# Differential attention: the sum of the two exponentials moves from VectorE to TensorE

## The reference

```python
q1, q2 = split(x @ w_q12);  k1, k2 = split(x @ w_k12);  v = x @ w_v     # each 512 x 128
diff = softmax(q1 @ k1.T * scale) - lam_full * softmax(q2 @ k2.T * scale)
out = diff @ v ;  out / rms(out) * (1 - LAMBDA_INIT)
```

## Time and profile before

| | |
|---|---|
| time, median of 3 runs | 976.47 us (974.27 to 980.98) |
| profiled execution, its own time | 976.01 us |
| span in that profile | 974.3 us |
| mean granted clock of TensorE | 0.942 |
| TensorE matmuls | 825.0 us busy, 85% |
| VectorE | 695.1 us busy, 71% |
| ScalarE | 552.2 us busy, 57% |
| GpSimd | 557.4 us busy, 57% |

### The profile page before, as it was taken

One profiled execution on the slowest core, in us unless ns is written; L12 is line 12 of the kernel. 1 busy time (PEld: TensorE's weight loads), 2 busy tenths in 40 slices (PEclk: granted clock), 3 DMA queues, 4 the chain that ended last, 5 costly groups with the idle time before them and its releaser, 6 DMA issues.

```text
span 974.3 us, 18283 instructions
## 1 busy us (share of the span) xinstructions
PE 825.0 (85%) x6646; PEld 542.3 (56%) x6646; DVE 695.1 (71%) x1441; ACT 552.2 (57%) x1027; POOL 557.4 (57%) x617
## 2 busy tenths in 40 slices
PE   7789998999899999999996877679788859999870
PEld 4356664448644444444443645445556549988870
DVE  5889984014798999999975599988576853654573
ACT  6566665440488887878884743436786544343220
POOL 2500006807188888888332599962077735878872
PEclk9899999999999999999998988789999979999995
DMA  5012210237021211121202992001011021232296
GB/s 160 1 44 87 87 44 23 65 130 206 13 44 37 30 30 35 35 36 35 35 14 62 167 285 84 1 1 43 1 48 53 28 94 43 89 99 65 89 247 206
DMA packets 109897, 70.62 MB, mean 72 GB/s; under 512 B 41538, under 2 KB 103436, under 8 KB 108272
## 3 DMA queue, kind: packets, MB, share of 16 engines
q1 hardware_dynamic: 99440, 60.11, 24.4%
q0 software_dynamic: 4608, 6.64, 2.1%
q10 hardware_dynamic: 5760, 2.70, 1.0%
HBM read 32.04 MB, written 31.60 MB: 65 GB/s over the span
## 4 chain that ended last, share of the span: by engine, by line
PE 37%; DVE 27%; POOL 13%; issue 10%; ACT 3%; DMA 2%; ACTq 1%; SPq 0%; POOLq 0%; DVEq 0%
PE banks L1975 5%; POOL y_dram L947 4%; DVE B_mneg L1122 4%; PE banks L1944 3%; PE banks L1921 3%; PE banks L1962 3%; PE banks L1894 3%; PE banks L1888 2%; DVE D_dmx L1238 2%; DVE C_nmax L1060 2%; PE banks L2045 2%; PE banks L1866 2%; PE banks L1949 2%; PE banks L2096 2%; PE banks L2003 2%
## 5 line engine op out<-in xcount | busy, mean ns | idle before, releaser
L1122 DVE TENSOR_REDUCE B_mneg<-banks 128x2 f32<-128x768 f32 (+1 forms) x128 | 136.4, 1086 | 7.7 <-PE banks L1949 4.0
L1637 ACT ACTIVATE B_pt<-banks 128x768 f32<-128x768 f32 (+1 forms) x128 | 117.1, 917 | 31.2 <-PE banks L1962 29.3
L785 POOL TENSOR_SCALAR_AFFINE_SELECT B_pt<-B_pt 128x512 f32<-128x512 f32 x128 | 80.4, 636 | 82.4 <-ACT B_pt L1637 62.6
L1768 ACT ACTIVATE F_gh<-banks 128x512 f32<-128x512 f32 (+1 forms) x96 | 49.4, 527 | 87.0 <-PE banks L2165 83.0
L902 POOL DMA_INDIRECT rows_dram<-F_xs,F_rowi x64 | 62.5, 977 | 59.6 <-issue 59.0
L1975 PE MATMUL banks<-B_pt,B_vp 128*32 128x512 f32 (+3 forms) x1024 | 95.6, 444 | 0.5 <-POOL B_pt L785 0.2
L2096 PE MATMUL banks<-D_qk 128*128 128x512 f32 x128 | 75.8, 677 | 10.2 <-DVE D_pr L1249 10.2
L947 POOL DMA_INDIRECT y_dram<-F_yo,F_ide x60 | 59.9, 998 | 37.8 <-DVE F_yo L1466 17.3
L2173 PE MATMUL banks<-F_gw,F_gh 128*128 128x128 f32 x640 | 75.3, 275 | 0.2 <-DVE F_yo L1466 0.2
L2173 PEld LDWEIGHTS banks<-F_gw,F_gh 128*128 128x128 f32 x640 | 73.9, 192 | 1.1 <-DVE F_yo L1466 0.4
L1944 PE MATMUL banks<-B_kt,B_qt 64*128 64x256 bf16 (+3 forms) x512 | 72.7, 301 | 1.7 <-ACT B_pt L1637 1.2
(11 more groups left out here) (300 smaller groups left out, 2228.3 us busy)
## 6 DMA issues: line engine op xcount, KB each, us to landing
comb_dram<-C_comb SPq DMA_DIRECT2D x6, 1024.0 KB, 3.9
rows_dram<-D_zeros SPq DMA_DIRECT2D x8, 650.0 KB, 15.5
F_xe<-rows_dram SPq DMA_DIRECT2D x8, 650.0 KB, 3.9
C_w<-w_in SPq DMA_DIRECT2D x16, 256.0 KB, 3.0
C_cst<-comb_dram SPq DMA_DIRECT2D x4, 1024.0 KB, 7.0
y_dram<-D_zeros SPq DMA_DIRECT2D x2, 2048.0 KB, 17.7
F_gw<-mw_in SPq DMA_DIRECT2D x16, 256.0 KB, 3.2
F_xs<-y_dram SPq DMA_DIRECT2D x16, 256.0 KB, 5.1
```

Source lines behind the costliest of these rows:

```text
L785: g.affine_select(out=w, in_=w, compare_op=ALU.is_ge, fill=0.0, base=0, pattern=[[0, G], [1, P]], channel_multiplier=-1).then_inc(B_md, 1)
L1122: v.tensor_reduce(mneg[:, g % 2, :, pairs[0], qt_], scores[:, :, 0:w], X, ALU.max, negate=True).then_inc(B_mx, 1)
L1637: a.activation(pt[:, 2 * hp:2 * hp + 2, PT_AT[kt]:PT_AT[kt] + w], scores[:, :, 0:w], ACT.Exp).then_inc(B_ex, 1)
```

## The change

The second exponential goes to SBUF as well (`pr2`). VectorE no longer forms the sum. It makes a 128x128 diagonal matrix `dmat` with c on the diagonal, as `lam_i` (the identity times -lam_full, made once) times s1 times 1/s2. TensorE turns E1 as before, by a transpose that opens a sum in PSUM, and adds E2 turned through the diagonal, as a float32 matmul of `pr2` with `dmat` in place of the identity. The PSUM bank of a second softmax is now free as soon as its exponential is taken, and the score tile waits for that instead of for `c`.

```diff
-                own.link(v.tensor_scalar(dco[:, t % 2:t % 2 + 1], dsum[:, u:u + 1], dinv[:, b % 2, t, 1:2], lms[:, 5:6],
-                                         ALU.mult, ALU.mult))
-                second = bank[2 + (D_PLAN.nth("s", "s", b, u + 1) - 1) % 3][:]
-                v.scalar_tensor_tensor(out=pr_[:, t, :], in0=second, scalar=dco[:, t % 2:t % 2 + 1],
-                                       in1=pr_[:, t, :], op0=ALU.mult, op1=ALU.add).then_inc(D_df, 1)
+                if b:
+                    dve.wait_ge(D_tf, D_PLAN.nth("T", "T", b - 1, t))
+                v.tensor_scalar(dmat[:, t, :], lam_i[:], dsum[:, u:u + 1], dinv[:, b % 2, t, 1:2], ALU.mult, ALU.mult
+                                ).then_inc(D_df, 1)
...
-                a.activation(pr_[:, u // 2, :] if u % 2 == 0 else scores, scores, ACT.Exp, bias=dmx[:, u:u + 1],
+                a.activation((pr_, pr2)[u % 2][:, u // 2, :], scores, ACT.Exp, bias=dmx[:, u:u + 1],
...
-                old = D_PLAN.back("s", ("s", b, u), 3)
-                if old and old[2] % 2:
-                    pe.wait_ge(D_df, D_PLAN.nth("c", "c", old[1], old[2] // 2))
-                elif old:
+                if n > 3:
                     pe.wait_ge(D_ex, n - 3)
...
-                    ins = t_.transpose(bank[1][:, m * P:(m + 1) * P], pr_[:, t, m * P:(m + 1) * P], ident[:])
+                    dst, keys = bank[1][:, m * P:(m + 1) * P], slice(m * P, (m + 1) * P)
+                    t_.matmul(dst, pr_[:, t, keys], ident[:], is_transpose=True, start=True, stop=False)
+                    ins = t_.matmul(dst, pr2[:, t, keys], dmat[:, t, :], start=False, stop=True)
```

More of the change, by code:

```diff
@@ L526, in build @@
         dmx, dsum = D1("dmx", [P, 8]), D1("dsum", [P, 8])
-        dinv, dco = D1("dinv", [P, 2, NT, 2]), D1("dco", [P, 2])
+        dinv = D1("dinv", [P, 2, NT, 2])
         dfT = D1("dfT", [P, 2, T])
+        pr2 = D1("pr2", [P, NT, T])
+        lam_i, dmat = D1("lam_i", [P, P]), D1("dmat", [P, NT, P])
         D_ln = sem("D_ln1_and_its_projection_in")
@@ L1244, in difference @@
                     dve.wait_ge(D_le, 3)
+                    own.link(v.tensor_scalar(lam_i[:], ident[:], lms[:, 5:6], None, ALU.mult))
                 own.link(v.reciprocal(dinv[:, b % 2, t, :], dsum[:, u:u + 2]))
-                own.link(v.tensor_scalar(dco[:, t % 2:t % 2 + 1], dsum[:, u:u + 1], dinv[:, b % 2, t, 1:2], lms[:, 5:6],
-                                         ALU.mult, ALU.mult))
-                second = bank[2 + (D_PLAN.nth("s", "s", b, u + 1) - 1) % 3][:]
-                v.scalar_tensor_tensor(out=pr_[:, t, :], in0=second, scalar=dco[:, t % 2:t % 2 + 1],
-                                       in1=pr_[:, t, :], op0=ALU.mult, op1=ALU.add).then_inc(D_df, 1)
+                if b:
+                    dve.wait_ge(D_tf, D_PLAN.nth("T", "T", b - 1, t))
+                v.tensor_scalar(dmat[:, t, :], lam_i[:], dsum[:, u:u + 1], dinv[:, b % 2, t, 1:2], ALU.mult, ALU.mult
+                                ).then_inc(D_df, 1)
             def outputs(b):
```

## The result

The changed kernel takes **985.84 us** (median of 14 runs, 978.11 to 990.93); the kernel before took 977.3 us beside it (14 runs, 974.27 to 981.72). The ratio is 1.0091, with a 95% interval of 1.0072 to 1.0109. The forecast was 977.5, with 969.5 to 983.5 as its range: the time lies above it. Ratios and their intervals, here and in the experiments, leave out executions over 1.5% above the fastest of their kernel, and medians are of all executions. The profiled execution took 987.99 us; its span is 986.2, 11.9 more than before.

A forecast was written before the change was run, and what follows sets the result against it. GpSimd's queue was taken to decide from 560 to 668 us and again from 708 us on. The terms 2.0 - 1.5 + 0.6 + 0.1 + 0.3 = +1.5 us on 976.0 gave 977.5, range 969.5 to 983.5.

The forecast's parts named there:

- part 2: VectorE's added work: `dmat` takes 0.28 us and waits 0.57 for GpSimd's running operation, so a tile saves only 0.20.
- fourth rival: Before 668 us `dmat` waits for more than GpSimd's running operation, 1.06 us longer per tile: +12.7, 990.2 us, chance 0.08.
- likeliest case: `dmat` waits for the GpSimd operation that runs, half of it on average: +1.5 us, 977.5 us, chance 0.50.
- A: 560 to 636 us: seven tiles each hold GpSimd for 0.28 us: +2.0 us.
- B: To the last group exponential: three tiles save VectorE time and TensorE gains half a clock effect: -1.5 us.
- C: The last v-products, 660 to 668 us: two tiles beside them hold GpSimd: +0.6 us.
- D: 668 to 708 us: a longer transposed tile on TensorE, +0.89, against VectorE's saving, -0.77: together +0.1 us.
- part 3: TensorE's added matmuls: 0.89 us per tile, 28.5 us over 32 tiles, mostly in gaps.
- E: The scatters: their 1.28 us spacing holds, 15 `dmat` beside them are longer: +0.3 us.
- the last term: Behind the scatters' stage: VectorE has 2.99 us to spare, so the last five tiles' delay is narrowly hidden: 0.
- no exclusion: `dmat` costs 0.28 us everywhere: -4.8, 971.2 us, chance 0.30; GpSimd's idle time caps the case at about -10.
- TensorE paces the router rounds: Added matmuls at 1.2 GHz lengthen the router rounds, VectorE saves nothing: +3.3 over the likeliest, 980.8 us, chance 0.12.

The follow-up runs named there:

- Experiment 4: The changed kernel with VectorE's diagonals in the accumulator-writing form, one 128x1 factor more per tile and no `lam_i`: 974.0 us, ratio 0.9986.
- experiment 2: The changed kernel without TensorE's added matmuls, so the second term is missing from the result: 988.2 us, ratio 1.0116.
- experiment 8: The kernel before with the second exponential in SBUF, so VectorE's sum reads both inputs from SBUF: 992.5 us, ratio 1.0109.
- 11: The changed kernel with accumulator-writing diagonals in all batches and without TensorE's second product, its term left out: 974.5 us, ratio 0.9978.
- experiment 1: The kernel before with TensorE's added matmuls alone, done with a zero matrix: 981.2 us, ratio 1.0050.
- experiment 9: The changed kernel with the accumulator-writing form for `lam_i` and the diagonals of batches 0 to 2 only: 977.0 us, ratio 0.9992.
- 12: The changed kernel with accumulator-writing diagonals, but in batch 3 VectorE adds out of PSUM with plain transposes: 975.4 us, ratio 0.9998.
- experiment 3: The changed kernel with ScalarE making `dmat` and VectorE only the 128x1 factor: 979.8 us, ratio 1.0055.
- 5: The changed kernel with accumulator-writing diagonals in batches 0 to 2 only, `lam_i` left as in the change: 985.9 us, ratio 1.0045.
- 6: The changed kernel with accumulator-writing diagonals in batches 3 to 7 only, `lam_i` left as in the change: 985.4 us, ratio 1.0037.
- 10: The kernel before with one operation more, an unread `lam_i` made once on VectorE at 569 us: 987.7 us, ratio 1.0075.

## Why the prediction was wrong

**The step that failed is in part 2: "an arrival at random waits half of the one running", 0.57 us, as the price of the exclusion.** The exclusion was read correctly from a single row, 0.08 us behind a memset. But behind that memset GpSimd had nothing queued. In the group part it mostly has, and VectorE's operation does not come next when the running one ends: it can be passed by one, two, five or nine more (two, three, six and ten with the running one). The twelve `dmat` up to 668.50 took 18.2 us together, 1.52 each, so 1.18 of waiting where I had 0.57, and one of them took 7.43. Three of the twelve were passed (2.40, 7.43 and 1.48). The other nine waited 0.43 in the mean, so the price was fair for them, and what it lacked is the few long waits. Every wait of three or more operations in these traces ended when GpSimd had nothing left to start; what decides which operation is passed stays open. `lam_i`, which I entered at 0.3, took 1.40 here and up to 10.81 elsewhere. Experiment 4 takes the lock away from both, at one 128x1 factor more per tile, and with it 12 us by the medians and 10 by the ratios; experiment 2 shows the loss without the added matmuls.

That is the mechanism of the **fourth rival** ("waits for more than the operation that runs"), which I gave 0.08. Its price was 1.06 us more per tile; measured is 0.61 more, plus `lam_i`. The time falls between the likeliest case and that rival (985.8, between 977.5 and 990.2). I weighed its evidence wrongly: I called the row weak, because nothing was queued behind the memset, and still took its 0.08 us as the evidence against. A row that lacks the condition of a rival can't speak against it.

The Trainium skill, "SBUF — State Buffer", section "Who interferes with whom", says that whoever issues first gets the shared pair for the whole instruction and the other fully blocks. The page's section "Summary: rules for kernel authors" says that the second one to issue blocks "until the first finishes". The traces agree on the block, and on two details of the first section: the form that writes its accumulator is exempt (experiment 4, 345 to 347 ns), and an operation with two SBUF inputs is not (experiment 8). They disagree on "until the first finishes": `lam_i` lasted 10.81 us, through ten operations.

By the terms:

- **A** (+2.0 forecast), **B** (-1.5) and **C** (+0.6) are the group part and sum to about +1; measured +5.6. A and C counted what `dmat` takes from GpSimd, 2.6 us in all. None of it shows: without its idle times GpSimd needs 89.7 us for the group part, before and after. The loss is the other way round: a blocked VectorE starves GpSimd (2.91, 4.88, 2.07 and 6.05 us of idle time, where the kernel before has 2.89 and 7.27 and nothing else over 1 us).
- **D** (+0.1): measured +4.9 for the router part. I had only T(3,0) ahead of the router's first link; T(3,1) is there too, 1.6 us in all up to the square root. The other 3.3 are the half clock from 697.4 to 709.4 us and one more T, less the 1.8 that come back. Of seven traces with the product in batch 3 the router part takes 51.1 us in the mean (48.3 to 53.0); of seven without, 48.9 (47.0 to 50.5). So the term was about +2 in the mean, and not +0.1. Single traces of one kind differ by up to 5, more than the effect, and the medians of 4 and 11 (974.0 and 974.5) don't show it; what the product costs once VectorE is free stays below what I can tell. Where VectorE is not free it cost 4.9 us (experiment 1), so "mostly in gaps" in part 3 was too kind as well; the two costs do not simply add up, since the change without the product is no faster (experiment 2).
- **E** (+0.3) and the last term (0): the scatters went as forecast, 80.79 us without a gap. Behind them 1.9 us came up that I did not find; 9, 11 and 12 show 186.8 to 187.3 us for that stretch too, 4 and the kernel before 185.6 and 185.5, so it is not the change's alone.
- **The rival "no exclusion"** (971.2): experiment 4 is this case made real, and it takes 974.0. The 7.2 us that the group part gains were forecast as 4.9 and the cap as 10; the router part gave most of it back in its trace.
- **The rival "TensorE paces the router rounds"** did not happen in the change. It is real where ScalarE has one more operation (experiment 3, 3.79 and 3.38 us).

Right were: the exclusion itself, T in 1.33 us, the waits of score tiles gone, the scatters' 81 us, and the signs that I had named for a wrong forecast ("`dmat` ... over 2", a first scatter 4 us or more off, though it came later and not earlier). GpSimd's stretch to its first wait did not get longer by 2 us; the wait came earlier, at 611.95.

## What to carry to other kernels

Beside an engine that runs back to back, give the other one forms that take no lock where it has work that the first will wait for: one operation of 0.35 us by its size lasted 10.81 us here, and its form alone made about 5 us of the kernel's time (experiments 5 and 9). Look at minimum, median and maximum of a group and not at its mean, and compare with what the other engine did until the exact end of the longest. The place of an operand (PSUM or SBUF) and the form of an instruction decide this, so a "free" move of an intermediate to SBUF is not free where GpSimd is the bound.

## What the runs showed of the hardware

- VectorE's 128x128 tensor-scalar, SBUF to SBUF, takes 345 ns, and up to 10.81 us beside a full GpSimd queue; the longest lasted through ten GpSimd operations. The form with an accumulator takes 345 to 347 ns (and 83 to read it) under the same load.
- The sum of two 128x512 tiles takes 751 to 752 ns with one input in PSUM, and up to 10.77 us with both in SBUF.
- Such waits are in the instruction's duration, so the engine reads as busy. Kernels with such operations before 668 us spread over 13 to 25 us from execution to execution (the change, experiments 2, 5, 6, 8, 10), those without over 3 to 11 (14 in experiment 9, which keeps the form beside the scatters).
- Transposes and float32 matmuls alternate at no extra cost: 0.11 and 0.22 us from start to start at 2.4 GHz.
- TensorE stayed at 1.2 GHz from 697.4 to 709.4 us although it was in use for 19.99 of 20 us from 700 on.
